# Four addresses made at once, product waits on the selectors, and a first transform with five slots

## The chip, the cores and the metric

The kernel runs on one core of one Trainium2 chip. A core has five engines that run side by side, each with its own stream of instructions, and they wait for each other through semaphores: TensorE (PE, products into the PSUM banks), VectorE (DVE), ScalarE (ACT), GpSimd (POOL) and SyncE (SP, which here only starts transfers). The metric is the device time of one execution in microseconds (us).

## The reference, cut to what matters

The model is a graph network of 1250 nodes with 512 features and 21250 edges, sorted by target. Its first layer is a relational convolution done twice: every edge sends its source's features, mixed with coefficients that hang on the edge's type and weight, to its target, and the sums are multiplied with four basis matrices. Two more layers (eight bases; a plain mean) and four blocks of graph attention follow.

```python
def _rel_graph_conv(h, src, dst, etypes, norm, basis, comp, bias, loop_w, apply_relu):
    hb = jnp.einsum('nd,bdo->bno', h, basis)
    coef = comp[etypes]
    m = coef[:, 0, None] * hb[0][src]
    ...
    m = m * norm[:, None]
    agg = jax.ops.segment_sum(m, dst, num_segments=n)
    out = agg + bias + h @ loop_w
...
h = _rel_graph_conv(emb, src, dst, etypes, edge_norm, basis0, comp0, bias0, loop0, True)
h = _rel_graph_conv(h, src, dst, etypes, edge_norm, basis1, comp1, bias1, loop1, False)
...
x = _layernorm(x + _L0_gnn_ref(...))      # two convolutions, 8 edge types, 4 bases
x = _layernorm(x + _L1_gnn_ref(...))      # one convolution, 32 edge types, 8 bases
x = _layernorm(x + _L2_gnn_ref(...))      # mean over the neighbours
x = _layernorm(x + _L3_gnn_ref(...))      # four attention blocks
```

## The kernel before

The kernel turns the convolution round: it first sums the source features by target and basis (`aggregate`), and then multiplies the sums with the bases (`transform`). Nodes are padded to 1280, which is NT = 10 tiles of 128; HALF is 5 tiles. KC = 4 is the number of 128-wide pieces of 512 features.

**An aggregation** (`aggregate`, called three times: L0a and L0b with 208 steps, L1 with 248) works through 168 tiles of 128 edges. POOL gathers each tile's source rows into a ring of 8 slots (L815). DVE makes a selector for every step, 8 steps ahead (`select`, L937), a 128 x 128 matrix that holds an edge's four or eight coefficients in the columns of its target. PE multiplies selector and gathered tile into one of four banks (L883, two instructions for a step). DVE adds the bank to the sum G of the step's window of targets (L986). Which slot a step reads and which window it adds to is known only on the chip: both engines read these numbers from tables, four steps (BATCH) with one load, into registers. Before, a register instruction (an ISA row in the orders below, FUSED_REGOPS in the trace) forms the address of every product and every sum just ahead of it, and on DVE this instruction carries the wait for the product. The fourth product and the first of the next four have the table's load between them (L818 on PE, L943 on DVE). A product also waits for the sum of four steps before, since there are four banks.

L0a also counts the edges between pairs of nodes for the attention: ACT makes signs (L911), DVE one-hot matrices (L951), PE multiplies them in between (L896, 328 products in 82 groups of four), and DVE adds each finished group (L960) and makes the one-hots of the group after the next. L0b has two pieces of work beside it: the next layer's coefficients, and the product of the hidden state with loop1 (`OwnProduct`). The sums are turned on PE at the end of L0a, and inside L0b and L1 (L860).

**A transform** (`transform`) takes 40 steps in the first call: two halves of five node tiles, five matrices (four bases and loop0), four pieces each. Step n needs the left sides split into a high and a low part (ACT L1386, then DVE L1414) and the weights split likewise (ACT L1388, then POOL L1455); PE then issues 15 products (L155 to L157). SP loads the weights four steps ahead (L1366, 256 KB each); before that, in the same queue, it writes the counts out (`CountStore.row`, L1082, ten transfers of 642 KB) and loads x (L1149) into the place where the counts stood, so the x load waits until they are written. `TransposeX` turns x for the last of the five matrices (L1158). `Hidden` is what follows each half: ReLU from the banks into a slot of h (L1224), turning on PE (L1210), the move into hT by ACT (L1227) or DVE (L1242), and the store to memory (L1201), which the gathers of L0b read. The second half can start once the banks are read. `half`, `middle` = 20 and `extra.at` = 16 are step numbers. The next aggregation's POOL work starts with a memset of G (L826), which stands in POOL's stream behind the last weight split.

## Time and profile before

| | us |
|---|---|
| median of 3 runs | 3152.34 |
| lowest and highest run | 3149.48, 3161.45 |
| the profiled execution | 3153.14 |
| its span, from first to last instruction | 3151.7 |
| PE busy | 2970.9 (94%) |
| DVE busy | 2072.5 (66%) |
| ACT busy | 1276.2 (40%) |
| POOL busy | 1168.5 (37%) |

### The profile page before, as it was taken

How to read it: one execution, taken by the hardware profiler on the slowest of the kernel's cores; microseconds unless marked ns; L12 is line 12 of the kernel's file. 1: busy time of each engine (PE TensorE's matmuls, PEld its weight loads, DVE VectorE, ACT ScalarE, POOL GpSimd, SP SyncE).
4: the chain of work that ended last, by engine and by line, in shares of the span. 5: the costliest groups of instructions: out<-in, count | busy, mean ns of one | idle time of the engine just before them, and what ended most of it. 6: DMA issues, size and time to landing. Idle time of an engine off the chain costs nothing.

```text
span 3151.7 us, 43512 instructions
## 1 busy us (share of the span) xinstructions
PE 2970.9 (94%) x14658; PEld 2181.5 (69%) x14658; DVE 2072.5 (66%) x5076; ACT 1276.2 (40%) x2250; POOL 1168.5 (37%) x938
## 2 busy tenths in 40 slices
PE   5999998999979889999999999999999999999999
PEld 2333775444843357875458998789987999789987
DVE  7999324887358853345377678567766776767777
ACT  4666432002340033342264454345542555435554
POOL 4666336665456643342012123511135101431022
PEclk8999998999989999999999999999999999999999
DMA  2555524565246642333013001310014001130012
GB/s 82 161 165 166 174 79 126 169 170 158 78 121 177 174 126 91 98 99 127 10 40 94 14 31 50 97 48 8 31 51 129 14 8 64 44 103 14 8 64 80
DMA packets 129580, 279.34 MB, mean 89 GB/s; under 512 B 22726, under 2 KB 45574, under 8 KB 128338
## 3 DMA queue, kind: packets, MB, share of 16 engines
q0 software_dynamic: 40320, 132.15, 14.9%
q1 hardware_dynamic: 87602, 141.76, 14.5%
q8 instruction: 124, 2.03, 0.3%
q10 hardware_dynamic: 1440, 2.62, 0.2%
q14 instruction: 94, 0.77, 0.1%
HBM read 227.85 MB, written 27.48 MB: 81 GB/s over the span
## 4 chain that ended last, share of the span: by engine, by line
PE 77%; DVE 14%; DMA 3%; issue 2%; ACT 2%; POOL 1%; SPq 1%; DVEq 0%; another core or an unknown queue 0%; POOLq 0%; ACTq 0%
PE bank L883 15%; PE bank L155 15%; PE bank L157 15%; PE bank L156 15%; PE bank L2483 5%; PE bank L2147 3%; DVE G L986 2%; PE bank L1787 2%; PE bank L860 2%; DVE y_tile L2099 1%; DVE y_tile L2101 1%; DVE x_stats L2082 1%; DVE x_L L2314 1%; PE bank L1055 1%; DMA yT_lo<-yT_new_lo 1%
## 5 line engine op out<-in xcount | busy, mean ns | idle before, releaser
L883 PE MATMUL bank<-gathered,selector 128*128 x1328 | 647.2, 614 | 65.9 <-DVE G L986 27.5
L986 DVE TENSOR_TENSOR G<-G,bank 128x512 f32 x664 | 449.8, 677 | 151.2 <-PE bank L883 133.1
L883 PEld LDWEIGHTS bank<-gathered,selector 128*128 128x128 f32 x1328 | 235.3, 194 | 323.3 <-issue 197.6
L2571 ACT CAST probT<-bank 128x512 fp32r<-128x512 f32 (+2 forms) x480 | 212.2, 516 | 263.5 <-PE bank L2483 262.6
L1455 POOL TENSOR_TENSOR weight_parts<-weight_ring,weight_parts 128x512 fp32r<-128x512 f32 x130 | 187.4, 1443 | 299.9 <-ACT weight_parts L1388 299.8
L2653 DVE CUSTOM_DVE_ANT_0 prob<-bank,count_by_src 128x512 f32<-128x512 f32 (+1 forms) x480 | 258.3, 588 | 59.0 <-PE bank L157 59.0
L1414 DVE TENSOR_TENSOR lhs_parts<-G,lhs_parts 128x640 fp32r<-128x640 f32 x122 | 102.4, 840 | 293.6 <-ACT lhs_parts L1386 293.4
L2579 DVE TENSOR_TENSOR probT<-bank,probT 128x512 fp32r<-128x512 f32 (+2 forms) x480 | 254.0, 585 | 52.3 <-ACT probT L2571 51.5
L870 ACT COPY G<-bank 128x512 f32<-128x512 f32 x160 | 82.0, 659 | 491.6 <-PE bank L860 445.9
L155 PE MATMUL bank<-weight_parts,lhs_parts 128*128 128x512 f32 x680 | 266.8, 392 | 12.7 <-POOL weight_parts L1455 8.0
L157 PE MATMUL bank<-weight_parts,lhs_parts 128*128 128x512 f32 x680 | 265.0, 390 | 0.0
L156 PE MATMUL bank<-weight_parts,lhs_parts 128*128 128x512 f32 x680 | 264.9, 390 | 0.0
L155 PE MATMUL bank<-probT,value_parts_hi 128*128 128x256 f32 (+3 forms) x800 | 234.5, 293 | 0.0
L2606 ACT ACTIVATE prob<-prob,negated_max 128x1250 f32<-128x1250 f32 x160 | 217.8, 1361 | 39.7 <-DVE negated_max L2660 39.7
L911 ACT ACTIVATE sign_src<-low_iota_16bit,src_low 128x321 bf16<-128x321 f16 x328 | 172.9, 560 | 124.8 <-PE bank L896 72.7
L157 PE MATMUL bank<-probT,value_parts_lo 128*128 128x256 f32 (+3 forms) x800 | 223.4, 279 | 0.0
L156 PE MATMUL bank<-probT,value_parts_hi 128*128 128x256 f32 (+3 forms) x800 | 222.9, 279 | 0.0
L2257 POOL TENSOR_TENSOR lhs_parts<-values_and_heads,lhs_parts 128x512 fp32r<-128x512 f32 x80 | 103.1, 1291 | 323.0 <-ACT lhs_parts L2310 322.6
L815 POOL DMA_INDIRECT gathered<-in_x,src_index x168 | 169.8, 1011 | 117.2 <-issue 47.1
L815 POOL DMA_INDIRECT gathered<-x_rows,src_index x168 | 162.3, 966 | 120.9 <-PE bank L883 72.7
L2483 PE MATMUL bank<-ident,prob 128*128 128x128 f32 (+1 forms) x1600 | 198.1, 271 | 4.7 <-DVE probT L2579 2.5
L815 POOL DMA_INDIRECT gathered<-hidden_rows,src_index x168 | 162.4, 967 | 93.0 <-PE bank L883 46.2
(294 smaller groups left out, 6802.9 us busy)
## 6 DMA issues: line engine op xcount, KB each, us to landing
weight_ring<-in_L_gnn_basis SPq DMA_DIRECT2D x64, 256.0 KB, 2.7
weight_ring<-in_L_gnn_bases SPq DMA_DIRECT2D x64, 256.0 KB, 2.6
x_L<-x_rows SPq DMA_DIRECT2D x50, 256.0 KB, 4.5
x_rows<-x_L SPq DMA_DIRECT2D x50, 256.0 KB, 5.7
yT_hi<-yT_new_hi SPq DMA_DIRECT2D x4, 2560.0 KB, 11.5
yT_lo<-yT_new_lo SPq DMA_DIRECT2D x4, 2560.0 KB
count_rows<-count SPq DMA_DIRECT2D x10, 642.0 KB, 7.9
count_by_dst<-count_rows SPq DMA_DIRECT2D x10, 642.0 KB, 4.8
```

The lines of the kernel that those rows point to most:

```text
L155: pe.matmul(acc, lhs[0], rhs[0], start=start, stop=False)
L156: pe.matmul(acc, lhs[0], rhs[1], start=False, stop=False)
L157: return pe.matmul(acc, lhs[1], rhs[0], start=False, stop=stop)
L815: pool.indirect_dma_start(xs[:, t % RING, :], None, rows, index).then_inc(*gathered[t % RING].inc())
L883: ins = pe.matmul(bank[s % banks][:], sel[:, s % SELECTORS, :], xs[:, ds(slot[s % BATCH], 1), :].rearrange("p t d -> p (t d)"), start=True ...
L986: ins = dve.tensor_tensor(g, g, bank[s % banks][:], ALU.add)
L1455: pool.tensor_tensor(weight_parts[:, n % 2, 1, :], ring[:, n % 4, :], weight_parts[:, n % 2, 0, :].bitcast(F32), ALU.subtract).then_inc(*w ...
L2483: ins = pe.transpose(bank[3 + q // 4][0:width, (q % 4) * P:(q % 4) * P + rows], prob[0:rows, t % 2, q * P:q * P + width], C.ident[0:rows, ...
L2571: ins = act.copy(hi, of)
L2579: ins = dve.tensor_tensor(lo, of, hi.bitcast(F32), ALU.subtract)
L2606: act.activation(prob[:, t % 2, :], prob[:, t % 2, :], ACT.Exp, bias=nmax[:, t % 2:t % 2 + 1], scale=scale, accum_out=rsum[:, h % 2, t:t + ...
L2653: dve.tensor_tensor_reduce(out=prob[:, s, c:c + width], in0=bank[n][:, 0:width], in1=count[:, t, c:c + width], scale=1.0, scalar=-2.0 * NE ...
```

## The change

There are four edits.

1. PE makes the addresses of four products at once (`batch`), behind the last product of the four before, and ahead of the counting products and the turns that follow it. The register instructions between the products are gone.
2. DVE makes the addresses of four sums at once (`addressed`), behind the fourth sum. The wait for the product of step s + 1 moves from the sum of that step to the instruction behind the sum of step s, which is a selector in all but the last steps. In L0a the count sum and the one-hots stand behind that selector. The selectors' own wait, for the product that last used their slot, is gone.
3. `TransposeX` loads and turns x in two halves, at steps 16 and 30 (`later`) in place of one at 16. SP issues one count transfer in a step over ten steps, in place of two in a step over five, and loads the halves of x at 15 and 22.
4. `Hidden` has five slots of h instead of two. ACT takes the ReLU of even tiles and moves odd ones, DVE the other way round. At the middle the turning of a tile stands between the products of step 20 (`beside_tile`) instead of ahead of them. Turned tiles use three banks instead of two.

```diff
+    def batch(b):
+
+        slots, tiles = (table(C.tile_of_step[path][0:1, b, w, :], PE, w, (RING - 1, T)[w]) for w in range(2))
+        rows = [xs[:, ds(slot, 1), :].rearrange("p t d -> p (t d)") for slot in slots]
+        for row in rows:
+            pe.lower_ap(row)
+        return rows, tiles
...
+        tile_rows_of, tiles = batch(0)
         for s in range(steps):
-            if s % BATCH == 0:
-                slot, tiles = (table(C.tile_of_step[path][0:1, s // BATCH, w, :], PE, w, (RING - 1, T)[w])
-                               for w in range(2))
             pe.wait_ge(tiles_landed.semaphore.sem, tiles[s % BATCH])
             pe.wait_ge(*selected(s + 1))
-            ins = pe.matmul(bank[s % banks][:], sel[:, s % SELECTORS, :],
-                            xs[:, ds(slot[s % BATCH], 1), :].rearrange("p t d -> p (t d)"), start=True, stop=True)
+            ins = pe.matmul(bank[s % banks][:], sel[:, s % SELECTORS, :], tile_rows_of[s % BATCH], start=True, stop=True)
             if s >= banks:
                 ins._wait_ge(*added(s - banks + 1))
             ins.then_inc(*multiplied.inc())
+            if (s + 1) % BATCH == 0 and s + 1 < steps:
+                tile_rows_of, tiles = batch((s + 1) // BATCH)
...
-    def windows_of(p, first, n):
-        return nc.values_load_multi_w_load_instructions(
+    def addressed(p, first, n, sums):
+
+        windows = nc.values_load_multi_w_load_instructions(
             C.window_of_step[p][0:1, first:first + n], engines=[DVE], min_val=0, max_val=p.windows,
             skip_runtime_bounds_check_because="a table that the chip has made of sorted nodes")[1]
+        places = [sums[:, ds(w, 1), :].rearrange("p w d -> p (w d)") for w in windows]
+        for place in places:
+            dve.lower_ap(place)
+        return places
+
+    def load_step(c):
+        return first_step[c] + ((first_step[c] + 1) % BATCH == 0)
...
+        sums = addressed(path, 0, BATCH, G)
+        dve.wait_ge(*multiplied(1))
         for s in range(steps):
             if s == cleared < path.windows + 1:
                 dve.wait_ge(*zeroed_act(1))
-            if s % BATCH == 0:
-                windows = windows_of(path, s, min(BATCH, steps - s))
             if counting and s < counting.first and s % CLEARED == 0:
                 dve.wait_ge(*zeroed_pool(s // CLEARED + 1))
-            dve.wait_ge(*multiplied(s + 1))
-            g = G[:, ds(windows[s % BATCH], 1), :].rearrange("p w d -> p (w d)")
+            g = sums[s % BATCH]
             ins = dve.tensor_tensor(g, g, bank[s % banks][:], ALU.add)
             if s:
                 ins._wait_ge(*added(s))
             ins.then_inc(*added.inc())
+            if (s + 1) % BATCH == 0 and s + 1 < steps:
+                sums = addressed(path, s + 1, min(BATCH, steps - s - 1), G)
+            if counting:
+                for c in range(0, PATHC.steps, 2):
+                    if load_step(c) == s:
+                        count_sums.update(zip((c, c + 1), addressed(PATHC, c, min(2, PATHC.steps - c), counting.count)))
+            if s + 1 < steps:
+                dve.wait_ge(*multiplied(s + 2))
             if s + AHEAD < steps:
                 select(s + AHEAD)
...
+        self.later = at + 3 * KC + 2
...
-            if extra and n == extra.at - 6:
-                extra.load()
-            if extra and 4 <= n < 4 + NT // 2:
-                for j in range(2 * (n - 4), 2 * (n - 4) + 2):
-                    C.count_store.row(j)
+            if extra and 4 <= n < 4 + NT:
+                C.count_store.row(n - 4)
+            if extra and n in (extra.at - 1, extra.later - 8):
+                extra.load(int(n >= extra.at))
...
             if extra and n == extra.at - 1:
-                extra.on_pe()
+                extra.on_pe(0)
+            if extra and n == extra.later - 1:
+                extra.on_pe(1, [epilogue.moved_tile(j) for j in (HALF - 2, HALF - 1)])
...
+                if j == HALF - 1:
+                    ins.then_inc(*multiplied.inc())
+                if n == middle:
+                    epilogue.beside_tile(j)
...
+        for j in self.tiles(half, 0):
+            self.wait_for_slot(act, j)
+            act.activation(self.h[:, j % HALF, :], C.bank[j % HALF][:], ACT.Relu).then_inc(*self.relued[0].inc())
+        for j in self.tiles(half, 1):
+            act.wait_ge(*self.turned(j + 1))
+            act.copy(*self.moved(j)).then_inc(*self.by_act.inc())
```

The first place is DVE's stream early in L0a, around one batch of four steps: `G` is the sum, `bank` the product, `multiplied_L0a` counts finished products. Before:

```order
L960 ISA [waits counted]
L960 TENSOR_TENSOR count_220<-count_220,bank 128x321 [waits count_added]
L951 TENSOR_TENSOR onehot_dst_218<-iota_61,place_in_window_70 128x512 [waits counted]
L943 TENSOR_LOAD window_of_step_58
L986 ISA [waits multiplied_L0a,G_zero_pool]
L986 TENSOR_TENSOR G_216<-G_216,bank 128x512 [waits added]
L937 SCALAR_TENSOR_TENSOR selector_5400<-iota_61,place_in_window_69,coef_L0a_72 128x128 [waits multiplied_L0a]
L986 ISA [waits multiplied_L0a]
L986 TENSOR_TENSOR G_216<-G_216,bank 128x512 [waits added]
```

And now:

```order
L996 TENSOR_TENSOR G_216<-G_216,bank 128x512 [waits added]
L948 TENSOR_LOAD window_of_step_58
L953 ISA x2
L941 SCALAR_TENSOR_TENSOR selector_5400<-iota_61,place_in_window_69,coef_L0a_72 128x128 [waits multiplied_L0a]
L971 TENSOR_TENSOR count_220<-count_220,bank 128x321 [waits counted,count_added]
L963 TENSOR_TENSOR onehot_dst_218<-iota_61,place_in_window_70 128x512 [waits counted]
L996 TENSOR_TENSOR G_216<-G_216,bank 128x512 [waits G_zero_pool,added]
L941 SCALAR_TENSOR_TENSOR selector_5400<-iota_61,place_in_window_69,coef_L0a_72 128x128 [waits multiplied_L0a]
L996 TENSOR_TENSOR G_216<-G_216,bank 128x512 [waits added]
```

The wait for the next product stood right ahead of the sum, with the selector, the count sum and the one-hots already done; now these three stand behind it. The register instructions of the single sums are gone, and the load has moved behind the fourth sum.

The second place is PE's stream at the middle of the first transform, from the last bias product on: `h` is the ReLU's output, `relued` counts finished ReLUs (of even tiles in the changed kernel, where `hidden` counts the odd ones). Before:

```order
L1481 MATMUL bank<-bias_row_parts_14729,ones_rounded_14730 128x512 x4
L1210 MATMUL bank<-ident_49,h_14724 128x128 [waits relued]
L1210 MATMUL bank<-ident_49,h_14724 128x128 x3
...
L1210 MATMUL bank<-ident_49,h_14724 128x128 [waits turned_by_act,relued]
L1210 MATMUL bank<-ident_49,h_14724 128x128 x3
L155 MATMUL bank<-weight_parts_14726,lhs_parts_14727 128x512 [waits relued,weight_lo,lhs_lo]
L156 MATMUL bank<-weight_parts_14726,lhs_parts_14727 128x512
```

And now:

```order
L1541 MATMUL bank<-bias_row_parts_14533,ones_rounded_14534 128x512 x4
L155 MATMUL bank<-weight_parts_14530,lhs_parts_14531 128x512 [waits relued,weight_lo,lhs_lo]
L156 MATMUL bank<-weight_parts_14530,lhs_parts_14531 128x512
L157 MATMUL bank<-weight_parts_14530,lhs_parts_14531 128x512
L1248 MATMUL bank<-ident_49,h_14528 128x128 [waits relued]
L1248 MATMUL bank<-ident_49,h_14528 128x128 x3
L155 MATMUL bank<-weight_parts_14530,lhs_parts_14531 128x512 [waits hidden]
```

The five turns stood in a block ahead of step 20; now each stands behind its own tile's three products in that step.

The third place is SP's queue in the same transform, which loads weights (`weight_ring`), writes the counts (`count_rows`) and loads x. Before:

```order
L1082 DMA count_rows<-count_220 128x4x321 x2
L1366 DMA weight_ring_14725<-in_L_gnn_basis 128x512 [waits weight_lo]
L1082 DMA count_rows<-count_220 128x4x321 x2
L1366 DMA weight_ring_14725<-in_L_gnn_basis 128x512 [waits weight_lo] x2
L1149 DMA x_14722<-in_x 128x10x512 [waits count_stored]
```

And now:

```order
L1098 DMA count_rows<-count_220 128x4x321
L1421 DMA weight_ring_14529<-in_L_gnn_basis 128x512 [waits weight_lo]
L1098 DMA count_rows<-count_220 128x4x321
L1421 DMA weight_ring_14529<-in_L_gnn_basis 128x512 [waits weight_lo] x2
L1171 DMA x_14526<-in_x 128x5x512 [waits count_stored]
```

One count transfer goes between two weights now, and the x load behind them is half as large and five steps later.

## Rows read from the trace of the kernel before

**Rows 1.** Costliest groups: busy, mean ns of one | idle before and its releaser.

```profile
L883 PE MATMUL bank<-gathered,selector 128*128 x1328 | 647.2, 614 | 65.9 <-DVE G L986 27.5
L986 DVE TENSOR_TENSOR G<-G,bank 128x512 f32 x664 | 449.8, 677 | 151.2 <-PE bank L883 133.1
```

**Rows 2.** Stages: window, us, busy (count) of PE, PEld, DVE, ACT, POOL, clock, DMA share, GB/s.

```profile
47.70:345.00 297.30, 268.43 (x905) 115.24 (x906) 266.68 (x581) 187.49 (x359) 177.74 (x175) 0.98 0.52 146
...
424.30:437.40 13.10, 10.06 (x41) 7.90 (x41) 2.21 (x3) 5.59 (x10) 1.42 (x1) 0.74 0.34 121
...
521.40:788.30 266.90, 255.99 (x843) 127.36 (x843) 211.62 (x452) 20.74 (x40) 160.57 (x167) 0.99 0.59 167
...
916.00:1211.40 295.40, 265.42 (x815) 127.33 (x816) 218.67 (x492) 59.98 (x79) 161.47 (x168) 0.97 0.54 152
```

**Rows 3.** Waits in the first half of the first transform: total, times, longest.

```profile
PE bank L155 <- POOL weight_parts L1455: 5.4, 4, 3.1
```

**Rows 4.** Chain of waits in the first transform: start, us, what.

```profile
361.94 10.10 DMA count_rows<-count
...
372.79 9.99 DMA weight_ring<-in_L_gnn_basis
...
407.63 0.73 ACT lhs_parts L1386
...
410.51 0.47 PE bank L155
```

**Rows 5.** DMA from 360 to 375 us.

```profile
DMA packets 3050, 4.27 MB, mean 285 GB/s; under 512 B 144, under 2 KB 2365, under 8 KB 3049
```

**Rows 6.** PE's timeline in the first transform: start, us, instruction.

```profile
402.01 4.86 PE L1158 MATMUL bank<-ident,x 128*128 128x128 f32 x40
...
424.33 1.42 PE L1481 MATMUL bank<-bias_row_parts,ones_rounded 33*128 33x512 f32 x5
...
437.41 0.39 PE L155 MATMUL bank<-weight_parts,lhs_parts 128*128 128x512 f32 x1
```

**Rows 7.** ACT's timeline at the middle of it.

```profile
425.79 0.60 ACT L1224 ACTIVATE h<-bank 128x512 f32<-128x512 f32 x1 [3.50 <-PE bank L1481]
```

**Rows 8.** POOL's and PE's timelines from the first transform into L0b.

```profile
498.09 17.60 POOL L826 MEMSET G<- 128x20992 f32 x1
515.86 1.17 POOL L815 DMA_INDIRECT gathered<-hidden_rows,src_index  x1 [0.16 <-issue]
521.41 2.07 PE L883 MATMUL bank<-gathered,selector 128*128 x2 [7.95 <-SPq L848]
```

**Rows 9.** The same at the start of L1.

```profile
912.43 1.09 POOL L815 DMA_INDIRECT gathered<-x_rows,src_index  x1 [6.83 <-DMA x_rows<-x]
916.10 1.22 PE L883 MATMUL bank<-gathered,selector 128*128 x1 [17.19 <-SPq L848]
```

**Rows 10.** DVE's timeline in L0a.

```profile
158.15 0.34 DVE L937 SCALAR_TENSOR_TENSOR selector<-iota,place_in_window,coef_L0a 128x128 f32<-128x128 f32 x1
158.41 0.47 DVE L960 TENSOR_TENSOR count<-count,bank 128x321 f32 x1
158.81 0.68 DVE L951 TENSOR_TENSOR onehot_dst<-iota,place_in_window 128x512 bf16<-128x512 f32 x1
159.41 0.67 DVE L986 TENSOR_TENSOR G<-G,bank 128x512 f32 x1
```

**Rows 11.** PE's timeline in the same stretch.

```profile
158.39 1.02 PE L883 MATMUL bank<-gathered,selector 128*128 x2
159.54 0.45 PE L896 MATMUL bank<-sign_src,onehot_dst 128*128 128x321 bf16 x2
160.61 1.12 PE L883 MATMUL bank<-gathered,selector 128*128 x2 [0.62 <-DVE selector L937]
```

**Rows 12.** L0a, 47 to 340 us: DVE's sums, with their idle time and its releasers.

```profile
L986 DVE TENSOR_TENSOR G<-G,bank 128x512 f32 x208 | 140.8, 677 | 14.7 <-PE bank L883 9.5 <-remote 4.7 <-issue 0.2
```

**Rows 13.** Waits in L0a: total, times, longest.

```profile
PEld bank L896 <- DVE onehot_dst L951: 47.5, 50, 6.0
```

More of the change, by code:

```diff
@@ L1141, in __init__, with tiles, load, on_pe @@
         self.C, self.x, self.xT, self.at = C, x, xT, at
+        self.later = at + 3 * KC + 2
         self.x_in = C.landed("x_in")
         self.turned, self.by_act, self.by_dve = C.event("x_turned"), C.event("xT_act"), C.event("xT_dve")
-    def load(self):
-        C = self.C
-        C.count_stored = C.count_store.stored.now()
-        C.sp.wait_ge(*C.count_stored)
-        C.sp.dma_start(self.x[:], C.A["x"].rearrange("(j p) d -> p j d", p=P)).then_inc(*self.x_in.inc())
-    def on_pe(self):
+    def tiles(self, part):
+        return range(part * HALF, (part + 1) * HALF)
+    def load(self, part):
+        C, sp = self.C, self.C.sp
+        if part == 0:
+            C.count_stored = C.count_store.stored.now()
+            sp.wait_ge(*C.count_stored)
+        rows = slice(part * HALF * P, (part + 1) * HALF * P)
+        sp.dma_start(self.x[:, part * HALF:(part + 1) * HALF, :],
+                     C.A["x"][rows, :].rearrange("(j p) d -> p j d", p=P)).then_inc(*self.x_in.inc())
+    def on_pe(self, part, free=()):
         C, pe = self.C, self.C.pe
-        pe.wait_ge(*self.x_in(1))
-        for j in range(NT):
+        pe.wait_ge(*self.x_in(part + 1))
+        for token in free:
+            pe.wait_ge(*token)
+        for j in self.tiles(part):
             if j >= 3:
@@ L1183, in __init__, with tiles, relued_tile, moved_tile @@
         self.C, self.h, self.hT, self.rows = C, h, hT, rows
-        self.relued, self.turned = C.event("relued"), C.event("tile_turned")
+        self.relued = C.event("relued"), C.event("hidden")
+        self.turned = C.event("tile_turned")
         self.by_act, self.by_dve = C.event("turned_by_act"), C.event("turned_by_dve")
-        self.stored = [C.landed(f"tile{s}_stored") for s in range(2)]
+        self.stored = [C.landed(f"tile{s}_stored") for s in range(HALF)]
     def done(self):
         return [self.by_act.now(), self.by_dve.now()]
+    def tiles(self, half, parity):
+        return [j for j in range(half * HALF, (half + 1) * HALF) if j % 2 == parity]
+    def relued_tile(self, j):
+        return self.relued[j % 2](j // 2 + 1)
+    def moved_tile(self, j):
+        return (self.by_dve, self.by_act)[j % 2](j // 2 + 1)
     def wait_for_bank(self, j):
-        self.C.pe.wait_ge(*self.relued(j + 1))
+        self.C.pe.wait_ge(*self.relued_tile(j))
     def on_sp_first(self):
@@ L1219, in on_act @@
         act.wait_ge(*self.summed(half + 1))
-        for j in range(half * HALF, (half + 1) * HALF):
-            if j >= 2:
-                act.wait_ge(*self.stored[j % 2](j // 2))
-                act.wait_ge(*self.turned(j - 2 + 1))
-            act.activation(self.h[:, j % 2, :], C.bank[j % HALF][:], ACT.Relu).then_inc(*self.relued.inc())
-            if j % 2 == 0:
-                act.wait_ge(*self.turned(j + 1))
-                act.copy(*self.moved(j)).then_inc(*self.by_act.inc())
+        for j in self.tiles(half, 0):
+            self.wait_for_slot(act, j)
+            act.activation(self.h[:, j % HALF, :], C.bank[j % HALF][:], ACT.Relu).then_inc(*self.relued[0].inc())
+        for j in self.tiles(half, 1):
+            act.wait_ge(*self.turned(j + 1))
+            act.copy(*self.moved(j)).then_inc(*self.by_act.inc())
     def between_on_act(self, o):
@@ L1237, in on_dve @@
     def on_dve(self, half):
-        dve = self.C.dve
-        for j in range(half * HALF, (half + 1) * HALF):
-            if j % 2:
-                dve.wait_ge(*self.turned(j + 1))
-                dve.tensor_copy(*self.moved(j)).then_inc(*self.by_dve.inc())
+        C, dve = self.C, self.C.dve
+        dve.wait_ge(*self.summed(half + 1))
+        for j in self.tiles(half, 1):
+            self.wait_for_slot(dve, j)
+            dve.tensor_scalar(self.h[:, j % HALF, :], C.bank[j % HALF][:], 0.0, None,
+                              ALU.max).then_inc(*self.relued[1].inc())
+        for j in self.tiles(half, 0):
+            dve.wait_ge(*self.turned(j + 1))
+            dve.tensor_copy(*self.moved(j)).then_inc(*self.by_dve.inc())
 class ResidualNorm:
@@ L1256, in wait_for_bank, with beside_tile @@
         self.C.pe.wait_ge(*self.added(j + 1))
+    def beside_tile(self, j):
+        pass
     def load(self, half):
@@ L1375, in on_act @@
         for n, (half, m, k) in enumerate(steps):
-            if extra and n == extra.at:
-                extra.on_act()
+            if extra and n in (extra.at, extra.later):
+                extra.on_act(int(n > extra.at))
             if n > middle:
@@ L1405, in on_dve @@
                 continue
-            if extra and n == extra.at:
-                extra.on_dve()
+            if extra and n in (extra.at, extra.later):
+                extra.on_dve(int(n > extra.at))
             if n > middle:
@@ L1548, in layers_0_1 @@
     xT = M.new("xT", [P, KC, NP])
-    h = M.new("h", [P, 2, D])
+    assert M.at <= M.end
+    M.at = tail - 4 * HALF * D
+    h = M.new("h", [P, HALF, D])
     M.at = after_G
```

69 lines of the change are left out of this document (37 added, 32 removed).

## The prediction

> **What bounds the kernel now.** I read the costliest groups first, then the busy time by stage, and only then the waits of the stages that the change touches. PE is the engine to follow: 94% busy, and outside the aggregations it has nothing to gain here. In the aggregations two groups face each other, PE's products and DVE's sums, and each waits for the other: 27.5 us of PE's idle time are put down to sums, 133.1 us of DVE's to products [rows 1]. By stage they are no twins. In L0a DVE is busy 266.7 of 297.3 us and bounds the stage; in L0b and L1 PE is busy 256.0 of 266.9 and 265.4 of 295.4 us, and DVE has 55 to 77 us to spare [rows 2]. So most of the 133 us is the idle time of an engine that does not bound, and is worth nothing. In L0a only 9.5 us of DVE's idle time come from products [rows 12]. The first transform has three places where PE stands: for weights in the first half (5.4 us in 4 waits, [rows 3]), at the middle, and at its end, up to the first product of L0b.
>
> **The first transform, first half.** PE's wait for weights is followed back in the chain: a count transfer takes 10.10 us to land, SP waits for it and issues x behind it, and the next weights need 9.99 us more [rows 4]. Sixteen DMA engines moved 285 GB/s meanwhile [rows 5]: the queue is full of bursts. Now ten counts of 642 KB and ten weights of 256 KB, 9.0 MB, are spread over ten steps. A step is 15 products; steps 15 to 19 lie between the first product behind the turned x at 406.6 (402.01 plus some 4.6 us for 40 turns) and the bias products at 424.33 [rows 6], 17.7 us, so 3.4 us each with the short stall behind the turns taken off. Over ten steps that is 264 GB/s, below the 285 shown, and x is 1.3 MB in place of 2.6, five steps later, with five steps until it is read. The waits go: 5.2 us (5.4 less some 0.2 that stand at 410.51, behind the turned x), and the slower restarts behind them bring it to 5.5. Bounds: 2 us, if counts and weights still meet, and 6.
>
> **The middle.** ACT starts the first ReLU at 425.79 [rows 7], and step 21 starts at 437.41 [rows 6], 11.6 us later. Now: PE starts step 20 as soon as the first ReLU is done, 0.65 us in. A tile costs it three products (3.4 / 5 = 0.68 us) and four turns (4 x 0.115 = 0.46 us, from 4.6 us for 40, [rows 6]), together 1.14. The turns end 6.4 us in. But ACT moves tile 3 before it prepares step 21: turned at 0.65 + 4 x 1.14 = 5.2, moved at 5.9 (a pass of ACT over a bank takes 0.6, [rows 7]). From ACT's left side to PE's next product it takes 2.9 us, as at 407.63 to 410.51 [rows 4]. Step 21 so starts 8.8 us in: 2.8 us gained, and what is late next is the preparation, not the ReLU. TensorE's clock was 0.74 in this stretch [rows 2], so part of it ran at 1.2 GHz, after PE had stood in pieces. The two waits that are left, 1.0 and 2.4 us, could lower it again, at up to 1.7 us for half a step at half speed. Bounds 1 and 4; I take 2.7.
>
> **x in two halves.** The 40 turns stay. Each block of turns is followed by a wait for the left side made of them (the block ended at 406.6, step 15 takes 3.4, and step 16 began at 410.51 [rows 4], 0.5 us late), and there are two blocks now. Cost 0.5 us, bounds 0 and 1.5.
>
> **The end of the transform.** Five slots let the last ReLUs, turns and stores run without waiting for stores; by the same prices they finish some 6 us sooner. I count nothing for it: the gathers of L0b stand behind POOL's memset of 17.60 us, which starts at 498.09 behind the last weights and ends at 515.69; the first gather starts at 515.86 [rows 8]. The memset doesn't move against PE's last steps. What is left is second hand: the load of loop1's weights is issued 6 us sooner and no longer shares the DMA engines with the first gathers. From first gather to first product it took 5.55 us here [rows 8] and 3.67 us at the start of L1 [rows 9]. Gain 1.9, bounds 0 and 2.
>
> The transform's sum: 5.5 + 2.7 - 0.5 + 1.9 = 9.6 us gained.
>
> **L0a.** DVE's own time per step doesn't shrink: its instructions start each other at 0.26 us (selector), 0.40 (count sum) and 0.60 (one-hots, as a sum) [rows 10], with the register instruction hidden behind them. What changes is when it waits. Before, the selector, the count sum and the one-hots, 0.26 + 0.40 + 0.60 = 1.26 us, were done ahead of the wait for the product; now they are behind it. Where PE is far enough ahead this costs nothing. It is not far ahead: in 50 of the 82 count groups PE waits for the one-hots [rows 13]. One case: one-hots start at 158.81, PE's count products at 159.54, 0.73 later. Without a load between, the next product could start at about 159.8 and be finished 1.1 us later [rows 11], 2.1 after the one-hots' start. DVE by then has done one-hots, sum, selector and sum: 0.60 + 0.60 + 0.26 + 0.60 = 2.06. The wait falls almost exactly where the product arrives. Upper bound of the loss: the selector uncovered in each of the 50 cases, 50 x 0.26 = 13 us. Against it stands the second edit: in this case the product did not start at 159.8 but at 160.61 [rows 11], since the two table loads stood between; behind the product before they would have been hidden. 0.8 us in about one case in four of the 50 is 10 us of PE's time, but of that DVE felt at most the 9.5 us of [rows 12], the bound on the side of a gain. The two nearly cancel. I take 2 us lost.
>
> **L0b and L1.** A DVE that has run dry now starts with a selector when the product arrives, then the sum: up to 0.26 us later. That reaches the end only where PE in turn waits for the sum, 22 times in the waits put down to it, 27.5 us in all, not all of them in these stages. 22 x 0.16 = 3.5, where 0.16 lies a little above halfway between no delay and the full selector, since a register instruction of the restart is gone too; I take 3. Bounds 0 and 14: all 65.9 us that PE stood ahead of products [rows 1], at the 1.25 us of a wait (27.5 / 22) some 53 waits, each 0.26 longer.
>
> Sum: 9.6 - 2 - 3 = 4.6 us gained. The profiled execution took 3153.14 us (span 3151.7), the median is 3152.34, so the two are the same within 0.8 us. From the median: 3152.3 - 4.6 = 3148 rounded.
>
> **Rivals.** A measurement of this kernel can tell about 0.5%, 15.8 us.
>
> *The aggregations gain.* The loads and register instructions sit on the circle product, sum, product more often than I count. For it: [rows 11], 0.8 us in one place; the waits for one-hots and sums. Then L0a gives its 9.5 us, and L0b and L1 about 5 in place of losing 3: 3152.3 - 9.6 - 9.5 - 5 = 3128. Against it: DVE has only 9.5 us to give in L0a. No row shows the gain, since the trace before has waits in one form only. 20%.
>
> *The circle closes in L0a, and the kernel is slower.* Place: DVE's wait for the product of step s + 1 behind the sum of step s. PE can't start that product before the one-hots, and DVE can't make the next one-hots before the product. Price: beyond the 0.26, the count sum and one-hots too come late in the half of the steps that have them, 0.26 + 0.4 x 1.0 = 0.66 us in each of the 50 cases, 33 us; L0b and L1 add 3. 3152.3 - 9.6 + 33 + 3 = 3179. It decides once the product arrives more than half a microsecond after the sum's end in these cases; by the one worked out it arrives about at its end plus the 0.26. 13%.
>
> *The transform doesn't gain.* Counts and weights still meet, the clock drops at the middle and at the second turning of x: 2 + 1 - 1.5 + 0 = 1.5 gained, 5 lost: 3156. For it: x and counts still go through one queue with the weights. 12%.
>
> The forecast itself has 55%, its own range 3141 to 3156.
>
> **Numbers.** Faster by over 0.5% (under 3136.6): the first rival and 2 of the forecast's 55, 0.22. Slower by over 0.5% (over 3168.1): the second rival and a rest, 0.14. Same: 0.64. For 8 in 10 the range reaches to the first rival and halfway to the second: 3128 to 3166.
>
> **What would show it.** The transform: no PE wait for weights in steps 6 to 9; steps 20 and 21 some 8.8 us apart from the first ReLU on; the first gather of L0b still directly behind the memset, and the first product 3.7 us later. L0a: DVE's idle time ahead of selectors, where there was none, between 10 and 20 us; over 35 us means the second rival, under 8 the first. L0b and L1: as long as before, within 5 us. I am wrong if the three aggregations together move by more than 15 us either way.

## The result, and the profile after

The changed kernel took 3145.4 us (median of 20 runs, 3138.6 to 3152.9) against 3154.3 us beside it (20 runs, 3148.3 to 3161.9): ratio 0.9968, 95% interval 0.9960 to 0.9976, about 10 us faster and within 0.5%. Its profiled execution took 3144.7 us, span 3143.3, 8.4 us less than the span before.

The stages of the changed kernel, in the columns of [rows 2]; the windows run from a stage's first instruction on PE:

```profile
48.25:341.20 292.95, 262.98 (x905) 113.65 (x906) 267.02 (x580) 188.71 (x359) 184.01 (x175) 0.98 0.52 148
...
422.80:427.80 5.00, 4.99 (x16) 4.02 (x17) 0.55 (x1) 0.00 (x0) 1.68 (x1) 0.69 0.34 105
...
509.10:776.00 266.90, 258.37 (x842) 127.30 (x842) 210.91 (x452) 20.93 (x40) 163.11 (x168) 0.98 0.59 168
```

PE's start times cut the span into stages that can be laid side by side. All figures of this table are differences of two such starts (first product of an aggregation, first split product of a transform), one profiled execution each:

| us | before | after |
|---|---|---|
| L0a with its turns | 297.1 | 292.7 |
| first transform, to L0b's first product | 176.5 | 168.1 |
| L0b | 266.9 | 267.6 |
| second transform, to L1's first product | 127.8 | 129.4 |
| L1 | 295.7 | 293.6 |
| all behind L1 | 1939.9 | 1943.7 |

The last row isn't touched by the change; in all fourteen traces of this study it lies between 1939.6 and 1943.9 with no order in it, so a difference of 4 us in one stage of one trace can be nothing. The transform's can't: it was 176.0 to 178.2 in the six traces that have the old transform, and 168.1 to 168.4 in the three that have the new one as it is in the changed kernel.

In the transform the waits for weights are gone (steps 6 to 9 take 3.40 us each). PE at the middle, in order of time (start, us, instruction, idle before and its releaser; the split products of L156 and L157 left out), answers to [rows 6]:

```profile
411.98 1.42 PE L1541 MATMUL bank<-bias_row_parts,ones_rounded 33*128 33x512 f32 x5
414.18 0.47 PE L155 MATMUL bank<-weight_parts,lhs_parts 128*128 128x512 f32 x1 [0.78 <-ACT h L1273]
...
419.48 0.60 PE L1248 MATMUL bank<-ident,h 128*128 128x128 f32 x4
...
422.81 0.77 PE L155 MATMUL bank<-weight_parts,lhs_parts 128*128 128x512 f32 x1 [2.73 <-POOL weight_parts L1510]
```

The first ReLU starts at 413.44. Step 21 starts at 422.81, 9.4 us later, behind a wait for its own preparation, and its first product takes 0.77 us in place of 0.39. The window row above shows why: the granted clock was 0.69 from 422.8 on, so part of step 21 ran at 1.2 GHz, and it took 4.95 us in place of 3.40. Over step 20, its wait included, the clock had still been 0.98. The kernel before, in the same columns, with its turns in the first row and its step 20 in the second:

```profile
425.00:433.00 8.00, 4.96 (x24) 3.75 (x23) 1.12 (x2) 3.86 (x7) 0.00 (x0) 0.69 0.37 136
433.00:437.40 4.40, 4.40 (x17) 3.58 (x16) 1.09 (x2) 1.73 (x3) 1.42 (x1) 0.79 0.34 111
```

Most of the slow stretch fell into the turns there, where PE waited anyway; its end cost step 20 some 1.0 us (4.37 in place of 3.40), and step 21 ran in 3.40.

At the end, POOL (answering to [rows 8]):

```profile
487.92 17.61 POOL L826 MEMSET G<- 128x20992 f32 x1
505.69 1.00 POOL L815 DMA_INDIRECT gathered<-hidden_rows,src_index  x1 [0.16 <-issue]
```

The last hidden rows are stored at 498.85; the gathers stand behind the memset for 6.8 us more, and the first product follows the first gather after 3.44 us (509.13), 5.55 before.

L0a: DVE's sums and selectors, with the idle time ahead of them, answering to [rows 12], and PE's products and count products:

```profile
L996 DVE TENSOR_TENSOR G<-G,bank 128x512 f32 x208 | 141.2, 679 | 0.1
L941 DVE SCALAR_TENSOR_TENSOR selector<-iota,place_in_window,coef_L0a 128x128 f32<-128x128 f32 x208 | 71.5, 346 | 9.7 <-PE bank L889 4.9 <-remote 3.3 <-issue 0.7
```

```profile
L889 PE MATMUL bank<-gathered,selector 128*128 x416 | 216.3, 605 | 1.9 <-DVE selector L941 1.9
L903 PE MATMUL bank<-sign_src,onehot_dst 128*128 128x321 bf16 x328 | 85.6, 306 | 28.6 <-DVE onehot_dst L963 21.1 <-issue 5.9 <-SPq L848 1.0
```

The same two PE groups of the kernel before:

```profile
L883 PE MATMUL bank<-gathered,selector 128*128 x416 | 220.3, 616 | 11.8 <-DVE selector L937 9.8 <-DVE G L986 1.4 <-SPq L848 0.5
L896 PE MATMUL bank<-sign_src,onehot_dst 128*128 128x321 bf16 x328 | 84.4, 306 | 17.6 <-DVE onehot_dst L951 11.4 <-issue 3.3
```

PE's idle time ahead of products has fallen by 9.9 us, that ahead of count products has grown by 11.0. A gain and a loss of one size stand side by side. It is tempting to put the gain down to the addresses and the loss to the moved wait; the experiments show that this is not how they divide.

### The profile page after: what moved, and what is told of

It reads as the page before. It is cut to its first block, busy times and chain, and to the rows that moved or that the text cites. A ratio compares the mean times of both kernels' runs of the same rounds, so it can differ in the third digit from the quotient of the medians.

```text
span 3143.3 us, 42911 instructions
## 1 busy us (share of the span) xinstructions
PE 2966.4 (94%) x14658; PEld 2176.8 (69%) x14658; DVE 2076.1 (66%) x5081; ACT 1275.2 (41%) x2245; POOL 1178.9 (38%) x938
## 3 DMA queue, kind: packets, MB, share of 16 engines
q1 hardware_dynamic: 87618, 141.76, 14.2%
## 4 chain that ended last, share of the span: by engine, by line
PE 74%; DVE 13%; another core or an unknown queue 6%; ACT 3%; issue 2%; DMA 2%; POOL 1%; DVEq 0%; SPq 0%; POOLq 0%; ACTq 0%
PE bank L155 16%; PE bank L157 16%; PE bank L156 16%; PE bank L889 9%; PE bank L2545 5%; PE bank L2209 3%; PE bank L1849 2%; PE bank L860 2%; DVE G L996 2%; DVE onehot_dst L963 1%; DVE y_tile L2161 1%; DVE y_tile L2163 1%; DVE x_stats L2144 1%; DMA yT_lo<-yT_new_lo 1%
## 5 line engine op out<-in xcount | busy, mean ns | idle before, releaser
L1469 DVE TENSOR_TENSOR lhs_parts<-G,lhs_parts 128x640 fp32r<-128x640 f32 x122 | 102.3, 840 | 288.4 <-ACT lhs_parts L1441 288.2
L157 PE MATMUL bank<-weight_parts,lhs_parts 128*128 128x512 f32 x680 | 266.5, 392 | 0.0
L156 PE MATMUL bank<-weight_parts,lhs_parts 128*128 128x512 f32 x680 | 266.5, 392 | 0.0
L157 PE MATMUL bank<-probT,value_parts_lo 128*128 128x256 f32 (+3 forms) x800 | 223.3, 279 | 0.0
L156 PE MATMUL bank<-probT,value_parts_hi 128*128 128x256 f32 (+3 forms) x800 | 222.9, 279 | 0.0
L815 POOL DMA_INDIRECT gathered<-in_x,src_index x168 | 176.5, 1050 | 107.6 <-issue 52.8
## 6 DMA issues: line engine op xcount, KB each, us to landing
yT_hi<-yT_new_hi SPq DMA_DIRECT2D x4, 2560.0 KB, 11.4
```

Source lines behind the costliest of these rows:

```text
L156: pe.matmul(acc, lhs[0], rhs[1], start=False, stop=False)
L157: return pe.matmul(acc, lhs[1], rhs[0], start=False, stop=stop)
L815: pool.indirect_dma_start(xs[:, t % RING, :], None, rows, index).then_inc(*gathered[t % RING].inc())
```

## The experiments

Each run is compared with the kernel before, run beside it. The three groups of four ran on different occasions and the kernel before took 3156.9, 3163.7 and 3099.3 us beside them, so only ratios and, with care, stages are carried from one group to another; ratios have 95% intervals. Of the kernel before there is one trace, from the first comparison, and none from the groups. Stage times are from one profiled execution of each kernel.

### First group: which half of the change, and where the wait stands

**aggregations_only** and **transform_only**: the two halves of the diff, each alone on the kernel before.

> Only the two edits of the three aggregations (addresses of four steps made at once behind a product or sum; DVE's wait for the next product ahead of the selector); the first transform as before. Theory A, mine: they are worth nothing here, 3154 us within 3, and what the changed kernel gained is its transform. Theory B: the 4.4 us that L0a was shorter in the changed kernel's trace (first product to first step of the transform 297.1 before, 292.7 after) come from these edits: 3149 to 3150 us, and L0a 4 to 5 us shorter than 297.1 here too.

> Only the edits of the first transform (x in two halves with the counts spread over ten steps, five slots for hidden rows); the aggregations as before. Theory A: the whole gain, 8.4 us from first step of the transform to first product of L0b (176.5 before, 168.1 after), so 3145.5 to 3147 us. Theory B: 3149 to 3150 us, since half of the gain is L0a's.

Measured: 3152.4, ratio 0.9984 (0.9976 to 0.9993), and 3149.2, ratio 0.9973 (0.9962 to 0.9985). The transform alone gives theory A of its own expectation: its stage takes 168.4 us, as in the changed kernel, and the kernel is 7.7 us faster by the medians, 8.5 by the ratio. The aggregations gain too, 2 to 8 us, so their theory A (nothing) fails; but the gain is not in L0a, as theory B had it: 294.7 us with the edits and 294.8 without, in two traces of one group. In which stage it lies isn't shown. So of the 4.4 us between the first two traces L0a owes at most a part to the change.

**wait_at_sum**:

```
-        dve.wait_ge(*multiplied(1))
 ...
+            dve.wait_ge(*multiplied(s + 1))
             g = sums[s % BATCH]
 ...
-            if s + 1 < steps:
-                dve.wait_ge(*multiplied(s + 2))
```

The selector's own wait for a free slot is back as well.

> The changed kernel with DVE's wait for the product back at the sum, and the selector's wait for a free slot back; addresses still made at once behind the sum. Theory A (the wait's place costs and gives nothing, since whoever waits for the product is late by the same product): 3145 us within 2, DVE's idle time ahead of selectors gone and ahead of sums in its place. Theory B (selector, count sum and one-hots uncovered behind the wait cost L0a time): 2 to 5 us faster than the changed kernel, 3140 to 3143. Theory C (a wait on a selector restarts sooner than one at the sum): 2 to 5 us slower, 3147 to 3150.

Measured: 3141.0, ratio 0.9949 (0.9937 to 0.9961). Theory B, by the length of L0a; the ratio's interval just touches that of the change (0.9960 to 0.9976). L0a takes 288.4 us, against 294.7 and 294.5 with the wait on the selector in the same group (aggregations_only and clearing_shared). PE's count products:

```profile
L903 PE MATMUL bank<-sign_src,onehot_dst 128*128 128x321 bf16 x328 | 85.3, 306 | 24.0 <-DVE onehot_dst L965 14.2 <-issue 8.1 <-SPq L848 1.0
```

The idle time put down to one-hots is 14.2 us here; with the wait ahead of the selector it is 21.1 in the changed kernel's trace, 24.2 and 19.0 in the two of this group. DVE's waits in all are 7.5 us ahead of sums and selectors, against 9.8 in the changed kernel. The one-hots come late where DVE waits for a product before it makes them.

**clearing_shared**: in the call of L0b, `PATH0.windows // 2` in place of `PATH0.windows + 1` for `cleared`. That is 20 windows for POOL and 21 for ACT (not 16 and 25, as the expectation says). DVE waits for ACT's part of this clearing at step 20.

> The changed kernel with POOL clearing 16 windows of G ahead of L0b's gathers in place of 41, and ACT the other 25 behind the transform. Theory A (the gathers stand behind the memset, 17.61 us from 487.92, while the last hidden rows are stored at 498.85): the first gather starts 6.6 to 6.8 us sooner and the kernel takes 3138 to 3139 us. Rival: something else is late at the same time (the stores, the loop's weights among the gathers, DVE waiting for ACT's windows at step 16): under 2 us gained.

Measured: 3141.7, ratio 0.9947 (0.9934 to 0.9960). The stage fell from 168.1 to 165.5, 2.6 us and not 6.7:

```profile
489.83 8.65 POOL L826 MEMSET G<- 128x10240 f32 x1
501.55 1.09 POOL L815 DMA_INDIRECT gathered<-hidden_rows,src_index  x1 [3.07 <-DMA hidden_rows<-h]
```

and the chain of waits behind it (start, us, what):

```profile
501.55 6.60 DMA gathered<-hidden_rows,src_index
508.23 2.08 PE bank L889 x2
```

The memset was what held the gathers: they now start 7.6 us behind the start of the bias products, 13.7 in the changed kernel. But 3.2 us are given back: the first gather lands after 6.60 us in place of 3.36, among the 1.3 MB of loop1's weights and bias rows that were issued at the same moment.

### Second group: each edit alone, and the middle

**wait_moved_alone**: only the wait moved, on the kernel before.

> The kernel before, with one edit: DVE's wait for the next product stands ahead of the selector, not of the sum; addresses as before. So far DVE's idle time between L0a's sums was 16.4 and 14.5 us with all as before, 12.7 to 14.7 with both edits and 8.7 with the addresses made at once alone. Theory A (the wait's move costs about 5 us of L0a by itself, whatever the addresses): idle 20 to 22 us, L0a 5 us longer than 295 to 297, 3154 + 5 = 3159 to 3162 us. Theory B (the move costs only where the addresses come early, and gives as much by its sooner restart where they don't): L0a within 2 us of before, 3154 within 3.

Measured: 3195.0, ratio 1.0096 (1.0080 to 1.0111), some 30 us slower, and L0a took 328.0 us. Both theories are wrong by far. DVE and PE in L0a:

```profile
L935 DVE SCALAR_TENSOR_TENSOR selector<-iota,place_in_window,coef_L0a 128x128 f32<-128x128 f32 x208 | 71.7, 347 | 21.4 <-PE bank L883 16.0 <-remote 4.5
...
L958 DVE TENSOR_TENSOR count<-count,bank 128x321 f32 x82 | 39.8, 486 | 14.6 <-issue 12.2 <-PE bank L896 2.1
```

```profile
L883 PE MATMUL bank<-gathered,selector 128*128 x416 | 221.3, 618 | 13.1 <-DVE selector L935 10.6 <-DVE G L985 2.0 <-issue 0.5
L896 PE MATMUL bank<-sign_src,onehot_dst 128*128 128x321 bf16 x328 | 85.4, 306 | 43.8 <-DVE onehot_dst L949 38.2 <-issue 5.6
```

DVE stands 12.2 us (36 times) ahead of count sums with nothing to wait for that the profile shows. The trace has it: in 32 of the 41 gaps of over 0.1 us there, a table load starts 0.01 us behind the selector (DVE's loads take 0.34 us or more in this trace), and the count sum follows it. The kernel before has no idle time ahead of its count sums. In none of the 27 waits of over 0.1 us ahead of selectors does a load start, and behind 21 of them one starts less than 0.2 us after the selector has started: the loads don't use the wait but stand behind it. The one-hots, which follow the count sum, come that much later, and PE waits 38.2 us for them, against 11.4 before. This is the circle of my second rival. That its 33 us are met (L0a is 31 longer) is luck in part, since no load stood in that price.

**pe_addresses_alone**: only `batch` and `on_pe` of the diff.

> The kernel before, with PE's table loads and addresses of four steps made behind the product and ahead of the count products, DVE unchanged. Theory A (the gain of the addresses is PE's: its idle time ahead of products, put down to selectors and sums, falls from 11.8 to about 2 us in L0a): DVE's idle time between L0a's sums falls from 16 to 8 or 9 us, L0a 6 to 8 us shorter, 3147 to 3149 us. Theory B (it is DVE's loads, which sat between its selector and its sum): L0a as before within 2 us, 3154 within 3.

Measured: 3154.3, ratio 0.9969 (0.9958 to 0.9981), 10 us faster; L0a 291.2 us. PE's products waited 1.8 us, as theory A had it. The sum's idle time fell from 14.7 to 10.7, not to 8 or 9. Theory A in the main, by the time and by L0a. PE's count products:

```profile
L904 PE MATMUL bank<-sign_src,onehot_dst 128*128 128x321 bf16 x328 | 85.6, 307 | 26.7 <-DVE onehot_dst L959 18.7 <-issue 5.8 <-SPq L848 1.5
```

Their idle time is 26.7 us with the wait still at the sum, 17.6 before and 28.6 in the changed kernel. So most of its growth by 11.0 us comes with PE's own addresses: PE is done with the products sooner and then stands ahead of the count products. That part is not the price of the moved wait. The sum of the two idle times (29.4 us before, 28.5 here) doesn't show the gain that the stage's length shows.

**prepare_first**:

```
-            if n > middle:
+            if n > middle and not isinstance(epilogue, Hidden):
                 epilogue.between_on_act(n - middle)
 ...
             act.copy(weight_parts[:, n % 2, 0, :], ring[:, n % 4, :]).then_inc(*weight_hi.inc())
+            if n > middle and isinstance(epilogue, Hidden):
+                epilogue.between_on_act(n - middle)
```

and the same on DVE.

> The changed kernel, but ACT and DVE prepare step 21 of the first transform ahead of their ReLUs and moves of the first five hidden rows. Theory A (what is late at the middle is ACT's preparation, asked for behind its move of tile 3): PE's wait of 3.0 us behind the turns of step 20 goes, the half-speed stretch of step 21 (4.95 us in place of 3.40) goes with it, the first ReLU starts up to 0.3 us later: from first ReLU to step 22 14.3 us becomes 10 to 11, and the kernel 3 to 4 us faster than the changed one, 3141 to 3142. Rival (POOL's weight rounding of 1.4 us or the banks of the turns are late all the same): under 1 us.

Measured: 3145.3, ratio 0.9944 (0.9931 to 0.9958), the stage 163.7 us, 4.4 less than after. ACT prepares step 21 beside the bias products; PE goes from the last turn to step 21 without a wait:

```profile
413.73 0.47 PE L155 MATMUL bank<-weight_parts,lhs_parts 128*128 128x512 f32 x1 [0.78 <-ACT h L1273]
...
419.38 0.47 PE L155 MATMUL bank<-weight_parts,lhs_parts 128*128 128x512 f32 x1
```

Steps 20 and 21 take 5.65 and 3.51 us in place of 8.63 and 4.95, with the clock at 1.00 throughout. 3.0 of the 4.4 us are step 20's, with its wait of 2.73, and 1.4 the clock.

**all_together**: wait_at_sum, clearing_shared and prepare_first in one, and loop1's weights issued behind the fourth landed gather, their products 12 steps later.

> The changed kernel with DVE's wait back at the sum, step 21 prepared first, the clearing of G shared with ACT (20 windows by POOL, 21 by ACT), and the load of loop1's weights put behind the fourth landed gather of L0b, its products 12 steps later. If the gains add: L0a 4 to 5, middle 3 to 4, start of L0b 6 (2.8 of the shared clearing and the 3.2 given back to slower gathers): 13 to 15 us under the changed kernel's 3145, 3130 to 3132 us. If they overlap or the late weights cost in L0b, 3134 to 3138.

Measured: 3139.7, ratio 0.9920 (0.9906 to 0.9934): 25 us under the kernel before by the ratio, 15 more than the change, as the first of the two expectations has it (its absolute times don't carry over to this group). The first product follows the first gather after 3.57 us again. But PE waits 3.24 us behind the seventh step, from 4 us after the weights were issued at 501.82, so this last edit is not shown to pay. Step 20 took 7.27 us here, with the clock at 0.77, against 5.65 in prepare_first, which has the same instructions there. So preparing step 21 first takes away the wait, but not every drop of the clock at the middle: the 1.4 us above are those of one pair of traces.

### Third group: what remained

**dve_edits_alone** (both of DVE's edits, PE as before) and **dve_addresses_alone** (the same with the wait at the sum).

> The kernel before with both of DVE's edits (addresses at once behind a sum, wait ahead of the selector) and PE as before. The wait's move alone made L0a 31 us longer (297.1 to 328.0), both edits with PE's addresses too left it at 292.7 to 294.7. Theory A (the 31 us are DVE's own loads, which behind the moved wait could no longer run while the product was made; taken out of its way by DVE's addresses at once): L0a 300 to 303 us, that is the 294 with all edits and the 6 to 7 that PE's edit is worth. Theory B (PE's two loads are what made it so long): L0a over 315 us.

> The kernel before with DVE's addresses made at once behind a sum, its wait at the sum, PE as before. PE's addresses alone made L0a 6.0 us shorter (297.1 to 291.2), both engines' 8.7 us (288.4). Theory A (DVE's loads were hidden behind its wait for the product): L0a 294 to 297 us, the kernel as before within 3 us. Theory B (DVE's own loads cost as much as PE's and the two overlap): L0a 290 to 292, 5 to 7 us faster than before.

Measured: 3113.5, ratio 1.0052 (1.0038 to 1.0065), and 3098.7, ratio 0.9996 (0.9987 to 1.0005). L0a took 304.6 and 290.3 us. The second is theory A by the time, in its own group: DVE's addresses alone bring nothing. Its L0a of 290.3 us would fit theory B, but the expected lengths came from other groups, and the aggregations are shorter in this one (the table below and the last section). With DVE's addresses and without PE's, the moved wait still costs 14.3 us in L0a, and 15 in all (3113.5 against 3098.7): between the two theories of the first, nearer to A. L0a by the place of the wait, us (a: first group, b: second, c: third):

| addresses at once | wait at the sum | wait ahead of the selector |
|---|---|---|
| none | 294.8 (a), 297.1 (first trace) | 328.0 (b) |
| on DVE | 290.3 (c) | 304.6 (c) |
| on PE | 291.2 (b) | not run |
| on both | 288.4 (a), 290.0 (b), 282.2 (c) | 294.7 (a), 292.6 (b), 287.8 (c) |

In every row and group the moved wait costs: 6.3, 2.6 and 5.6 us with both, 14.3 without PE's addresses, and some 30 without any (by the kernel's time in its own group; in L0a 31 to 33 against traces of others). The addresses made at once save 6 to 8 us where the wait stays (6.4 with both in group a, 8.1 for PE's alone in group c), and are what makes the move bearable.

**counts_burst**: two counts per step from step 4 to 8 as before, all else of the change kept.

> The changed kernel, but the ten counts of 642 KB are issued two per step from step 4 to 8, as before, with x still five steps later and in halves. Theory A (spreading the counts is what took away PE's waits for weights in steps 6 to 9): all 5 to 6 us of them are back. Theory B (half of it was SP's wait for the last count ahead of x, with the weights of the steps behind it): steps 6 and 7 lose 2 to 3 us again, step 9 nothing, so 2 to 3 us more than the changed kernel.

Measured: 3094.3, ratio 0.9988 (0.9979 to 0.9997). Steps 6 to 9 took 3.51, 5.44, 3.50 and 3.40 us, 2.25 lost and none in step 9. Theory B: the longest of the old waits (3.3 us, in step 9) did not come back with the burst. What is left for it is SP's wait for the counts ahead of x, which went because x is asked for later, half at a time; later and halved were not tried apart. The stage is 4.0 us longer, 172.2; of the 1.8 beyond the burst 1.6 stand in step 20:

```profile
409.20:419.30 10.10, 7.41 (x35) 5.96 (x35) 4.49 (x6) 4.20 (x8) 1.97 (x2) 0.83 0.45 157
```

The same 1.6 us stand in step 20 of all_together, which has no burst, so they are the clock's and not shown to be the burst's.

**three_edits**: all_together without the late weights.

> As all_together, but the load of loop1's weights and its products stand where they were. If the late load brought its 3.2 us, this is 3 us slower than all_together, ratio to before 0.993; if it cost in L0b what it brought (L0b was 271.4 us there, 3.8 of them in one wait of PE right behind the first products), the two are the same within 2 us.

Measured: 3079.1, ratio 0.9936 (0.9922 to 0.9949). The interval overlaps with that of all_together; whether the late weights pay stays open. In the stage they do: with its slow step 20 set aside (1.6 us) all_together's 159.4 us would be 157.8, some 3.1 less than here. What L0b gives back can't be told across groups. The stage is 160.9 us, the 168.1 less the 4.4 and the 2.6 of its two edits, so these add.

## Why the prediction was right, and where it was wrong

The forecast of 3148 us was 3 us off, and its sum of 4.6 us gained stands against about 9. That is luck in two ways. It started from a median of 3152.3, and the kernel before took 3154.3 when run 20 times, which hid 2 us of the missing gain. And its terms miss in both directions: the middle gave 2.0 less than forecast, the aggregations together 11 more, while the stages that no term covers (the second transform and all behind L1) came out 5.4 longer in this pair of traces. Nothing shows that these 5.4 us come from the change.

- **First half of the transform**: 5.5 us predicted, 5.9 measured (steps 6 to 9 took 19.5 us together, and take 13.6 now; none of the waits of [rows 3] is left). Right, except that two causes lay in it: the counts' burst (2.25), and by elimination SP's wait in front of x (the rest), which counts_burst told apart.
- **The middle**: this step failed. "Step 21 so starts 8.8 us in" was nearly right (9.4): ACT's left side started 6.0 us in, against 5.9, but from there it took 3.35 us and not 2.9, as POOL's part of the weights took 1.88 us in place of 1.41. That "what is late next is the preparation, not the ReLU" was shown by prepare_first. But I took 2.7 us for the gain and the clock only as a bound: counted to the start of step 22, 15.0 us became 14.3 and the gain is 0.7. The clock fell at the end of the wait in step 20, and the slow time came to lie on step 21, where before most of it lay on a wait. The bound that I named, 1.7 us for half a step at half speed, is what happened (1.55).
- **x in halves**: 0.5 predicted, 0.4 measured (the 40 turns with the stalls around them cost 5.23 us before, 5.65 after, beyond the 3.40 of each step that holds them).
- **The end**: 1.9 predicted, 2.1 measured; the memset still held the gathers, for 6.8 us, and clearing_shared shows both parts of that sentence, the cover and the collision with loop1's weights. Sum of the transform: 9.6 predicted, 8.4 measured.
- **L0a**: 2 us lost predicted, 0 (one group) to 4.4 (the first two traces) gained. That two effects nearly cancel is right, and both show alone: the addresses gain 6 to 9 us (L0a 288.4 against 294.8 and 297.1), where I had 9.5 as the bound, the wait costs 3 to 6, where I had 13. DVE's idle time ahead of selectors was 9.7 us, just under the 10 to 20 named. Two readings beneath the terms were wrong. The first is that DVE "bounds the stage": the same row of [rows 2] has PE busy 268.4 us and DVE 266.7, and the gain of the addresses is PE's (alone 10 us; DVE's alone nothing). The second is "in 50 of the 82 count groups PE waits for the one-hots": the 50 waits of [rows 13] are those of weight loads, which overlap the products, and PE's products themselves waited for one-hots 14 times, 11.4 us. The 13 us and the second rival's 33 both multiply by 50. I also did not see that without the addresses the wait's move would have closed the circle in full.
- **L0b and L1**: 3 us lost predicted, 1.4 gained, within the 5 named and within what one trace can tell.
- **Rivals**: that the circle closes in L0a was real, but for another kernel (wait_moved_alone, 31 us in L0a). The mechanism that I priced at 33 us needs DVE's own loads behind the wait; the change moves them away in the same stroke. The Trainium skill has it ("Perfetto Trace Analysis", "Per-engine timelines") that an instruction of DVE waits in a wait queue while the sequencer goes on to the next. The shorter restart that I worked out from it shows as a gain in no run: in all three pairs the kernel with the wait ahead of the selector is the slower. How long a restart takes in either form was not measured by itself. Nor did the sequencer use these waits for its table loads: in the traces of wait_moved_alone, dve_edits_alone and the changed kernel, no load of DVE's starts inside any of the 75 waits of over 0.1 us ahead of L0a's selectors.

## What to carry to other kernels

Where two engines wait for each other in turn, put a wait behind all the work that doesn't need it: a selector that could have been made during the wait delays not only the sum but everything that follows it. Table loads and address instructions belong behind an instruction that gives cover, and moving a wait without them can turn a hidden load into the bound of the stage. When a stall is shortened, follow it to the end of the next full step, since a clock that falls at the end of the stall is paid for in the work behind it. Idle time that moves from one group of instructions to another is no gain or loss yet; compare the distances of starts.

## What the hardware showed

L1, which is the same instructions in all kernels but for the address and wait edits, took 293 to 296 us in the first group, 298 to 302 in the second and 259 to 261 in the third; L0b 267 to 272, 270 to 274 and 255 to 258. Everything behind L1 was the same within 4.3 us in all. The loss is mostly in waits between the engines, and it is spread over the whole of the loop. DVE's selectors in L1, in the changed kernel and in counts_burst (third group), in the columns of [rows 1]:

```profile
L941 DVE SCALAR_TENSOR_TENSOR selector<-iota,place_in_window,coef_L 128x128 f32<-128x128 f32 x240 | 82.6, 344 | 66.8 <-PE bank L889 58.5 <-remote 4.8 <-issue 3.3
```

```profile
L941 DVE SCALAR_TENSOR_TENSOR selector<-iota,place_in_window,coef_L 128x128 f32<-128x128 f32 x248 | 91.3, 371 | 37.2 <-PE bank L889 33.8 <-DMA x_rows<-x 3.1 <-issue 0.2
```

PE's side of it: its products stood 15.5 us for DVE's sums in the first trace, 0.5 in the second. DVE itself was not faster in the second, as a selector took 371 ns there and 344 in the first. So some 35 us of L1 belong neither to the program nor to its edits but to where or when it ran, and they are larger than all that was changed here. The record has each group on a chip of its own (14, 9 and 4), so chip and occasion can't be told apart. Their cause was not found.
